# A gated delta-rule decoder layer on one core: the level-64 products of the triangular inverse issued in pairs, gate projections between the groups

## The chip, the cores and the metric

The kernel runs on one core of a Trainium2 chip, in fp32 throughout. The metric is the device time of one execution in microseconds; lower is better.

## The reference

A decoder layer on x of 4 sequences of 256 tokens, width 256: x plus an attention part, plus a cross-attention mix, plus a mixture of experts. The change lies in the attention part, a recurrence over 8 heads of width 128 with two key and value pairs for each token:

```python
def step(state, inp):
    q_t, k_t, v_t, b_t, g_t = inp
    state = state * jnp.exp(g_t)[..., None, None]
    for j in range(nh):                      # nh = 2
        kj = k_t[:, j]
        corr = jnp.einsum('bhk,bhkv->bhv', kj, state)
        u = (v_t[:, j] - corr) * b_t[:, j][..., None]
        state = state + jnp.einsum('bhk,bhv->bhkv', kj, u)
    o_t = jnp.einsum('bhk,bhkv->bhv', q_t, state)
    return (state, o_t)
...
gate = (x @ Wg).reshape(B, L, H, Dh)
o = o * jax.lax.rsqrt(jnp.mean(o * o, axis=-1, keepdims=True) + EPS)
o = o * norm_w * jax.nn.silu(gate)
out = o.reshape(B, L, H * Dh) @ Wo
```

q, k and v are projections of x, each with a causal convolution of 4 taps and a silu.

## The kernel before, in words

The recurrence is worked in chunks of 64 tokens (128 key rows, since each token has two), 16 chunks for each head. In a chunk the dependence of the 128 corrections on each other is a unit triangular 128x128 matrix, and its inverse is needed. The inverse is built by levels. Blocks of 32x32 on the diagonal are inverted on GpSimd. From them TensorE builds blocks of 64 (items p32 and t32: two products), and from those the full 128 (items x32, p64, t64). In the last three, for every chunk, x32 is a turn (transpose) of a 64x64 block, p64 a 64x64 product with that turned block, and t64 a second 64x64 product with the result. Each item comes as n = 0 and n = 1, of eight chunks each; all eight write one PSUM bank, and ScalarE copies the bank out (to XP for x32 and p64, to TT for t64). p64 n waits for the copy of x32 n, and t64 n for the copy of p64 n.

Five engines each run a program of their own, written out by hand and tied by semaphores. `run_heads` walks through steps; in step s, stage A works on head s (projections, convolutions, norms), stage B on head s − 1 (Gram matrices, decays, inverse), stage C on head s − 2 (the scan over the chunks), stage E on head s − 3 (output projection). Steps 3 to 7 hold all four; step 8 has no stage A. A step has 12 slots. In each slot TensorE does one phase of the scan (slots 0, 3, 6, 9: keys times state, L686; then TT products, L700; then outputs, L714 and L715, with the state update, L719), then the fill items of that slot, then a norm (L610) where there is one, then one projection (L581, slots 0 to 9). After slot 11 comes the place `LAST`, and the next step begins with `FIRST`: the Gram matrices (L637) and q times k (L640).

The table `FILL` sets which items stand where, and every engine walks through the same table. Among the items are gate (one half of the gate's projection of the head, L589: two matmuls of 512 columns, then silu on ScalarE, L860), kend (four turns, L642, evacuated by VectorE, L1131), and out (output projection, L749). Fill items take three PSUM banks in turn: an item waits until the item three before it in the order has been evacuated (`bank_free`).

On VectorE a slot is: first tap of the convolution of the projection before (L1053; it waits for ScalarE's copy L836), the scan's part (R, L1153; U, L1161; S, L1170), the two other taps, the fill items. At the end of slot 9 it turns the 32x32 blocks into X1 (L1143), which p32 (L666) reads in slot 10. In step 8, without projections, the threshold search for the cross attention (L1068, L1070) stands ahead of those turns.

An fp32 matmul appears in the trace as two matmul instructions, each with a weight load of its own; a turn appears as one.

Of the kernel before, what the change touches and what calls it, by code (L numbers as in the profile page):

```python
# [17 lines left out]
STEPS = 64  # L18
CH = SEQ // STEPS
# [79 lines left out]
def four(kind):  # L99
# [15 lines left out]
        9: {"B": [("gate", 0)]},  # L115
        10: {"B": [("p32", 0), ("p32", 1)], "E": [("out", 3)]},
        11: {"B": [("t32", 0), ("t32", 1), ("kend", 2)]},
        LAST: {"B": [("x32", 0), ("x32", 1), ("gate", 1), ("p64", 0), ("p64", 1), ("t64", 0), ("t64", 1)]}}
# [43 lines left out]
def attention(nc, ctx, t, dram):  # L162
# [370 lines left out]
    def tensor_program(pe):  # L533
# [80 lines left out]
        def item(kind, n, X):  # L614
# [12 lines left out]
            if kind in ("gram", "qk", "vtok", "kend"):  # L627
# [19 lines left out]
                return  # L647
            if kind == "p32":
# [4 lines left out]
            elif kind == "x32":  # L653
                pe.wait_ge(t32_done, 2 * h + n + 1)
            elif kind == "p64":
                pe.wait_ge(x32_done, 2 * h + n + 1)
            else:
                pe.wait_ge(p64_done, 2 * h + n + 1)
            for k in range(BC // 2):
                m = n * (BC // 2) + k  # L660
                a_m, t_m = aT[:, m // CH, m % CH, :], TT[par][:, m // CH, m % CH, :]
                cols = slice(k * STEPS, (k + 1) * STEPS)
                if kind == "p32":
                    for g in range(2):
                        src, out = slice(2 * g * NB, (2 * g + 1) * NB), slice((2 * g + 1) * NB, (2 * g + 2) * NB)
                        last = mm(bank[out, k * NB:(k + 1) * NB], a_m[src, out], X1[src, m, :], start=True, stop=True)  # L666
                elif kind == "t32":
                    for g in range(2):
                        src, out = slice((2 * g + 1) * NB, (2 * g + 2) * NB), slice(2 * g * NB, (2 * g + 1) * NB)
                        last = mm(bank[out, k * NB:(k + 1) * NB], P32[src, m, :], t_m[src, src], start=True, stop=True)  # L670
                elif kind == "x32":
                    last = nc.tensor.transpose(bank[0:64, cols], t_m[0:64, 0:64], ident[0:64, 0:64])
                elif kind == "p64":
                    last = mm(bank[64:128, cols], a_m[0:64, 64:128], XP[0:64, m, :], start=True, stop=True)  # L674
                else:
                    last = mm(bank[0:64, cols], XP[64:128, m, :], t_m[64:128, 64:128], start=True, stop=True)
            last.then_inc(b_mm, 1)
# [1339 lines left out]
```

## Time and profile before

| | |
|---|---|
| median of 3 runs | 946.26 us (945.72 to 947.09) |
| profiled execution | 951.51 us, span 949.5 us |
| TensorE matmul busy | 849.2 us, 89% of the span |
| TensorE weight load busy | 597.6 us, 63% |
| VectorE busy | 527.4 us, 56% |
| ScalarE busy | 391.3 us, 41% |
| GpSimd busy | 348.5 us, 37% |
| mean granted clock of TensorE | 0.946 |

Times in the trace count from the start of the span. The head loop fills the first two thirds of it; the mixture of experts, the rest. A steady step of the head loop is about 67 us long. Weight loads run beside matmuls, so their busy time does not add to that of the matmuls. In the rows, an idle time in square brackets is what the engine waited directly before the instruction, and the name behind it is what ended the wait; a row without brackets began with no idle time to speak of. The granted clock is 1.00 at 2.4 GHz and 0.50 at 1.2 GHz.

### The profile page before, as it was taken

How to read it: one execution, taken by the hardware profiler on the slowest of the kernel's cores; microseconds unless marked ns; L12 is line 12 of the kernel's file. 1: busy time of each engine (PE TensorE's matmuls, PEld its weight loads, DVE VectorE, ACT ScalarE, POOL GpSimd, SP SyncE). 2: the span in 40 equal slices, each digit the busy share in tenths (PEclk: the TensorE clock that was granted, in tenths of full speed). 3: DMA queues.
4: the chain of work that ended last, by engine and by line, in shares of the span. 5: the costliest groups of instructions: out<-in, count | busy, mean ns of one | idle time of the engine just before them, and what ended most of it. 6: DMA issues, size and time to landing. Idle time of an engine off the chain costs nothing.

```text
span 949.5 us, 16704 instructions
## 1 busy us (share of the span) xinstructions
PE 849.2 (89%) x5816; PEld 597.6 (63%) x5817; DVE 527.4 (56%) x1221; ACT 391.3 (41%) x839; POOL 348.5 (37%) x654
## 2 busy tenths in 40 slices
PE   4869999999999999999999876874999999999992
PEld 3344566766766856866667765763666677667762
DVE  3664747878868868878778764465511111111113
ACT  2736746655654654565565323102222222222220
POOL 0158268357555564573682570003330000000005
PEclk9987999999999999999999995797999999999997
DMA  8221230131031021021201301009563001100104
GB/s 206 73 41 27 72 81 8 17 78 17 9 79 23 11 70 23 13 67 24 51 2 23 90 1 28 1 1 374 213 223 134 28 28 33 33 29 26 33 23 127
DMA packets 102595, 57.91 MB, mean 61 GB/s; under 512 B 64192, under 2 KB 98048, under 8 KB 102528
## 3 DMA queue, kind: packets, MB, share of 16 engines
q1 hardware_dynamic: 99488, 51.62, 19.8%
q0 software_dynamic: 1536, 4.20, 1.4%
q10 hardware_dynamic: 1504, 1.20, 0.4%
q8 instruction: 41, 0.67, 0.3%
q14 instruction: 26, 0.21, 0.1%
HBM read 42.45 MB, written 14.55 MB: 60 GB/s over the span
## 4 chain that ended last, share of the span: by engine, by line
PE 76%; DVE 10%; ACT 6%; issue 4%; POOL 2%; DMA 1%; SPq 0%; POOLq 0%; ACTq 0%; DVEq 0%
PE bank L1598 16%; PE bank L581 13%; PE bank L1643 9%; PE bank L715 3%; PE bank L589 3%; DVE y L1053 3%; PE bank L749 3%; PE bank L640 3%; PE bank L700 3%; PE bank L719 2%; PE bank L714 2%; PE bank L595 2%; PE bank L1630 2%; PE bank L674 2%; PE bank L686 2%
## 5 line engine op out<-in xcount | busy, mean ns | idle before, releaser
L1053 DVE SCALAR_TENSOR_TENSOR y<-bank,cwh,y 128x510 f32<-128x510 f32 (+2 forms) x240 | 177.6, 744 | 78.9 <-ACT y L836 75.2
L581 PE MATMUL bank<-xnT,wbuf 128*128 128x512 f32 x320 | 165.2, 642 | 5.3 <-DVE y L1053 4.7
L1598 PE MATMUL bank<-f_wgu,f_xgT 128*128 x368 | 118.8, 466 | 0.0
L1857 DVE TENSOR_TENSOR f_act<-f_sg,bank 128x352 f32<-128x352 f32 x62 | 32.2, 521 | 143.8 <-PE bank L1598 141.4
L1369 POOL TENSOR_TENSOR term<-inv,blk 128x126 f32<-128x126 f32 (+22 forms) x248 | 87.8, 354 | 43.9 <-DMA blk<-a_blocks 25.1
L1932 POOL DMA_INDIRECT f_back<-slots_y,f_slot x16 | 15.4, 963 | 231.4 <-DMA slots_y<-f_yb 224.8
L581 PEld LDWEIGHTS bank<-xnT,wbuf 128*128 128x128 f32 x320 | 57.4, 199 | 66.8 <-issue 53.7
L1372 POOL TENSOR_TENSOR inv<-inv,term 128x126 f32<-128x126 f32 (+22 forms) x248 | 91.6, 369 | 19.4
L1705 ACT ACTIVATE f_sg<-bank 128x352 f32<-128x352 f32 x62 | 28.7, 464 | 161.0 <-PE bank L1598 152.7
L1643 PE MATMUL bank<-f_wdn,f_actT 128*128 (+1 forms) x372 | 91.5, 388 | 0.9 <-ACT f_actT L1718 0.8
L1598 PEld LDWEIGHTS bank<-f_wgu,f_xgT 128*128 128x128 f32 x368 | 66.2, 190 | 36.8 <-issue 7.6
L836 ACT ACTIVATE y<-bank,cwh 128x512 f32<-128x512 f32 x80 | 54.9, 686 | 74.8 <-PE bank L581 73.3
L1643 PEld LDWEIGHTS bank<-f_wdn,f_actT 128*128 128x128 f32 x372 | 67.9, 189 | 24.5 <-issue 12.0
L1314 POOL TENSOR_TENSOR dx<-dx,minus_beta 128x1024 f32<-128x1024 f32 x8 | 15.2, 1903 | 131.9 <-DVE beta_n L1103 131.9
L930 ACT ACTIVATE vtok<-bank,kn 128x128 f32<-128x128 f32 x128 | 36.5, 369 | 32.6 <-PE bank L645 32.5
L715 PE MATMUL bank<-mq,R 128*128 128x64 f32 x256 | 46.4, 279 | 2.8 <-DVE R L1161 2.8
L1299 POOL TENSOR_TENSOR factor<-factor,masks 128x8 f32<-128x8 f32 x8 | 13.3, 1664 | 96.3 <-DVE factor L1205 96.3
L1598 PE MATMUL bank<-f_wgu,f_x2T 128*128 128x352 f32 x128 | 44.6, 495 | 0.4 <-DVE f_act L1857 0.4
L715 PEld LDWEIGHTS bank<-mq,R 128*128 128x128 f32 x256 | 38.6, 197 | 6.0 <-DVE R L1161 3.0
L1869 DVE COPY f_yb<-bank 128x256 f32<-128x256 f32 x23 | 9.8, 425 | 53.0 <-PE bank L1643 53.0
L700 PEld LDWEIGHTS bank<-R,TT 128*128 128x128 f32 x192 | 25.0, 193 | 22.1 <-issue 19.3
L595 PE MATMUL bank<-gm,masks 64*128 64x512 f32 x64 | 27.5, 687 | 12.1 <-ACT dx L870 8.0
(208 smaller groups left out, 1585.2 us busy)
## 6 DMA issues: line engine op xcount, KB each, us to landing
f_wgu<-in_exp_gu SPq DMA_DIRECT2D x8, 1408.0 KB, 8.6
f_wdn<-in_exp_dn SPq DMA_DIRECT2D x8, 640.0 KB, 9.7
blk<-a_blocks SPq DMA_DIRECT2D x16, 256.0 KB, 3.9
slots_x<-oT SPq DMA_DIRECT2D x24, 128.0 KB, 1.8
f_xg<-slots_x SPq DMA_DIRECT2D x24, 128.0 KB, 2.0
slots_y<-f_yb SPq DMA_DIRECT2D x23, 128.0 KB, 1.7
a_blocks<-aT SPq DMA_DIRECT2D x64, 32.0 KB, 1.6
inverses<-inv SPq DMA_DIRECT2D x16, 128.0 KB, 3.0
```

The costliest lines, as they stand in the source:

```text
L581: last = mm(bankA[p % 2][:, :], wbuf[A.par][:, kt, wblk, :], xnT[:, kt, (p % 2) * 512:(p % 2 + 1) * 512], start=kt == 0, stop=kt == 1)
L595: return mm(bank[:, :], mask("rest" if kind == "dx" else "ones", i * STEPS, STEPS), gm[half_, :, :].rearrange("p n t -> p (n t)"), start=T ...
L700: last = mm(bankC[1][:, b * P:(b + 1) * P], TT[par][:, b, c, :], R[:, b, :] if c else vtok[par][:, b, c, :], start=True, stop=True)
L715: last = mm(out, U[:, b, :], mq[par][:, b, c, :], start=c == 0, stop=True)
L836: a(y[p % 2][:, :, :].rearrange("p b t -> p (b t)"), bankA[p % 2][:, :], ACT.Copy, scale=cwh[A.par][:, cb, 3:4]).then_inc(evac_done, 1)
L930: last = a(vtok[B.par][:, b, c, :], bank[:, c * P:(c + 1) * P], ACT.Copy, scale=kn[:, b * CH + c:b * CH + c + 1])
L1053: v.scalar_tensor_tensor(out=y[p % 2][:, :, k:], in0=src[:, :, 0:SEQ - k], scalar=cwh[A.par][:, cb, 3 - k:4 - k], in1=y[p % 2][:, :, k:], ...
L1369: g.tensor_tensor(step_term, inv[:, 0:r, j:j + 1].to_broadcast([P, r, k]), blk[:, j:j + 1, j + 1:].to_broadcast([P, r, k]), ALU.mult).then ...
L1372: g.tensor_tensor(inv[:, 0:r, j + 1:], inv[:, 0:r, j + 1:], step_term, ALU.add).then_inc(inv_done if j == NB - 2 else inv_step, 1)
L1598: last = mm(gu[c][:, 0:FFH], xt[:, k, :], wgu[:, e, k, at:at + FFH], start=k == 0, stop=k == 1)
L1643: last = mm(dn[par][:, 0:HID], aT[0:rows, par, k, :], wdn[0:rows, e, k, :], start=k == 0, stop=k == FT - 1)
L1857: v.tensor_tensor(av[:, par, half * FFH:(half + 1) * FFH], sg[:, half, :], gu[2 * half + 1][:, 0:FFH], ALU.mult).then_inc(f_act, 1)
```

## The change

The three items of level 64 keep their work, but not their order. x32 1 and p64 0 are issued together, chunk by chunk in turn, and so are p64 1 and t64 0 (`joined`); each pair first makes all the waits of both items, and raises both semaphores at its end. Between the groups stand other items: gate 0 comes from slot 9 to between x32 0 and the first pair, gate 1 stands between the pairs, kend 2 comes from slot 11 to between the second pair and t64 1. The other engines follow the same table: ScalarE copies the gate's half 0 in `LAST`, and VectorE evacuates kend 2 in `LAST`.

```diff
-        9: {"B": [("gate", 0)]},
+        9: {},
         10: {"B": [("p32", 0), ("p32", 1)], "E": [("out", 3)]},
-        11: {"B": [("t32", 0), ("t32", 1), ("kend", 2)]},
-        LAST: {"B": [("x32", 0), ("x32", 1), ("gate", 1), ("p64", 0), ("p64", 1), ("t64", 0), ("t64", 1)]}}
+        11: {"B": [("t32", 0), ("t32", 1)]},
+        LAST: {"B": [("x32", 0), ("gate", 0), ("x32", 1), ("p64", 0), ("gate", 1), ("p64", 1), ("t64", 0), ("kend", 2), ("t64", 1)]}}
+JOIN = {("x32", 1): ("p64", 0), ("p64", 1): ("t64", 0)}
...
+        def joined(first, second, X):
+
+            banks = [bankB[bank_of(kind, X.h, n)] for kind, n in (first, second)]
+            for kind, n in (first, second):
+                bank_free(pe, kind, X.h, n)
+                level_ready(kind, n, X.h)
             for k in range(BC // 2):
...
+                one_, two_ = level(*first, X, k, banks[0]), level(*second, X, k, banks[1])
+            one_.then_inc(b_mm, 1)
+            two_.then_inc(b_mm, 1)
...
                         for kind, n in items:
-                            item(kind, n, stages[stage])
+                            if (kind, n) in JOIN:
+                                joined((kind, n), JOIN[kind, n], stages[stage])
+                            elif (kind, n) not in JOIN.values():
+                                item(kind, n, stages[stage])
```

`level` and `level_ready` hold the products and the waits that stood in `item` before:

```python
if kind == "x32":
    last = nc.tensor.transpose(bank[0:64, cols], t_m[0:64, 0:64], ident[0:64, 0:64])
elif kind == "p64":
    last = mm(bank[64:128, cols], a_m[0:64, 64:128], XP[0:64, m, :], start=True, stop=True)
else:
    last = mm(bank[0:64, cols], XP[64:128, m, :], t_m[64:128, 64:128], start=True, stop=True)
```

The order on TensorE in slots 9 and 10 of step 6, before (L686 is the scan's product of slot 9, L589 gate 0, L666 level 32's first products):

```order
L686 MATMUL bank<-S,kT 128x128 x4
L589 MATMUL bank<-xnT,wg 128x512 x2
L610 MATMUL bank<-osq,masks 32x128 x4
L581 MATMUL bank<-xnT,wbuf 128x512 x2
L700 MATMUL bank<-R,TT 128x128 x4
L666 MATMUL bank<-X,aT 32x32 x32
```

And in the changed kernel, whose line numbers are other ones (L707 is L686 of before, L676 is L666):

```order
L707 MATMUL bank<-S,kT 128x128 x4
L611 MATMUL bank<-osq,masks 32x128 x4
L582 MATMUL bank<-xnT,wbuf 128x512 x2
L721 MATMUL bank<-R,TT 128x128 x4
L676 MATMUL bank<-X,aT 32x32 x32
```

The gate's two matmuls have gone from between the scan's product and the products of level 32.

The order on TensorE at the end of the same step, before (from t32, L670, to the next head's Gram matrices, L637):

```order
L670 MATMUL bank<-TT,P 32x32 x32
L642 MATMUL bank<-masks,kT 128x128 x4
L610 MATMUL bank<-osq,masks 32x128 x8
L672 MATMUL bank<-masks,TT 64x64 x16
L589 MATMUL bank<-xnT,wg 128x512 x2
L674 MATMUL bank<-XP,aT 64x64 x16
L676 MATMUL bank<-TT,XP 64x64 x16
L637 MATMUL bank<-kraw 128x128 x16
```

And in the changed kernel (L680 is t32, L682 the turns, L684 p64, L686 t64, L643 kend, L590 gate); each pair of alternating rows stands eight times, and only its first and last are shown:

```order
L680 MATMUL bank<-TT,P 32x32 x32
L611 MATMUL bank<-osq,masks 32x128 x8
L682 MATMUL bank<-masks,TT 64x64 x8
L590 MATMUL bank<-xnT,wg 128x512 x2
L682 MATMUL bank<-masks,TT 64x64
L684 MATMUL bank<-XP,aT 64x64
...
L590 MATMUL bank<-xnT,wg 128x512 x2
L684 MATMUL bank<-XP,aT 64x64
L686 MATMUL bank<-TT,XP 64x64
...
L643 MATMUL bank<-masks,kT 128x128 x4
L686 MATMUL bank<-TT,XP 64x64 x8
L638 MATMUL bank<-kraw 128x128 x16
```

A second gate projection and the turns of kend now stand among the level's items, and four of its six items are issued in turns instead of in blocks.

## Rows read from the trace of the kernel before

**Rows 1.** Timeline of TensorE, slots 9 and 10 of a steady step: start, duration, instruction.

```profile
441.18 1.05 PE L686 MATMUL bank<-S,kT 128*128 128x128 f32 x8
442.07 1.88 PE L589 MATMUL bank<-xnT,wg 128*128 128x512 f32 x4
443.88 0.43 PE L610 MATMUL bank<-osq,masks 128*32 128x128 f32 x8
444.24 1.98 PE L581 MATMUL bank<-xnT,wbuf 128*128 128x512 f32 x4
...
447.04 1.20 PE L666 MATMUL bank<-X,aT 32*32 32x32 f32 x64
```

**Rows 2.** Timeline of VectorE at the same place.

```profile
442.10 0.75 DVE L1053 SCALAR_TENSOR_TENSOR y<-bank,cwh,y 128x510 f32<-128x510 f32 x1 [0.27 <-ACT y L836]
...
445.24 1.42 DVE L1143 STREAM_TRANSPOSE X<-TT 32x512 f32<-32x512 f32 x2
446.98 0.75 DVE L1053 SCALAR_TENSOR_TENSOR y<-bank,cwh,y 128x510 f32<-128x510 f32 x1 [0.32 <-ACT y L836]
```

**Rows 3.** Timeline of TensorE, end of the same step.

```profile
450.96 1.20 PE L670 MATMUL bank<-TT,P 32*32 32x32 f32 x64
452.10 0.66 PE L642 MATMUL bank<-masks,kT 128*128 128x128 f32 x4
452.68 0.65 PE L610 MATMUL bank<-osq,masks 128*32 128x128 f32 x16
453.26 1.08 PE L672 MATMUL bank<-masks,TT 64*64 64x64 f32 x16
454.27 1.98 PE L589 MATMUL bank<-xnT,wg 128*128 128x512 f32 x4
456.18 2.08 PE L674 MATMUL bank<-XP,aT 64*64 64x64 f32 x32
458.10 2.05 PE L676 MATMUL bank<-TT,XP 64*64 64x64 f32 x32
460.07 2.94 PE L637 MATMUL bank<-kraw 128*128 128x128 f32 x24
```

**Rows 4.** Timeline of ScalarE at the same end: copies of t32 0 and p64 1.

```profile
452.09 0.38 ACT L942 ACTIVATE TT<-bank 32x256 f32<-32x256 f32 x1
...
458.29 0.59 ACT L946 ACTIVATE XP<-bank 64x512 f32<-64x512 f32 x1 [0.34 <-PE bank L674]
```

**Rows 5.** The instructions of line 551: duration min/median/max, first and last start.

```profile
L551 PE MATMUL bank<-wab,xnT x64: 270/281/303, 16.1 to 19.5; 128*64 128x24 f32 x64
```

**Rows 6.** Timeline of TensorE in step 8.

```profile
579.88 1.92 PE L666 MATMUL bank<-X,aT 32*32 32x32 f32 x64 [7.37 <-DVE X L1143]
...
588.89 1.11 PE L642 MATMUL bank<-masks,kT 128*128 128x128 f32 x4
589.93 1.91 PE L672 MATMUL bank<-masks,TT 64*64 64x64 f32 x16
591.77 3.78 PE L589 MATMUL bank<-xnT,wg 128*128 128x512 f32 x4
595.49 3.35 PE L674 MATMUL bank<-XP,aT 64*64 64x64 f32 x29
598.53 0.36 PE L676 MATMUL bank<-TT,XP 64*64 64x64 f32 x1
598.63 0.31 PE L674 MATMUL bank<-XP,aT 64*64 64x64 f32 x1
...
603.83 0.66 PE L728 MATMUL bank<-osq,masks 128*32 128x256 f32 x4 [1.63 <-ACT osq L887]
```

**Rows 7.** TensorE by stretches: from:to and length, busy (instructions), clock, DMA share, GB/s.

```profile
54.00:55.00 1.00, 0.00 (x0) 1.00 0.00 0
...
590.00:603.00 13.00, 12.21 (x85) 0.50 0.00 0
606.00:610.00 4.00, 4.00 (x27) 0.84 0.03 6
```

More of the change, by code:

```diff
@@ L647, in item, with level_ready @@
                 return
+            level_ready(kind, n, h)
+            for k in range(BC // 2):
+                last = level(kind, n, X, k, bank)
+            last.then_inc(b_mm, 1)
+        def level_ready(kind, n, h):
             if kind == "p32":
@@ L658, in item @@
                 pe.wait_ge(p64_done, 2 * h + n + 1)
-            for k in range(BC // 2):
[L660 to L676, printed above, removed]
@@ L677, in item, with level @@
-            last.then_inc(b_mm, 1)
+        def level(kind, n, X, k, bank):
+            par, m = X.par, n * (BC // 2) + k
+            a_m, t_m = aT[:, m // CH, m % CH, :], TT[par][:, m // CH, m % CH, :]
+            cols = slice(k * STEPS, (k + 1) * STEPS)
+            if kind == "p32":
+                for g in range(2):
+                    src, out = slice(2 * g * NB, (2 * g + 1) * NB), slice((2 * g + 1) * NB, (2 * g + 2) * NB)
+                    last = mm(bank[out, k * NB:(k + 1) * NB], a_m[src, out], X1[src, m, :], start=True, stop=True)
+            elif kind == "t32":
+                for g in range(2):
+                    src, out = slice((2 * g + 1) * NB, (2 * g + 2) * NB), slice(2 * g * NB, (2 * g + 1) * NB)
+                    last = mm(bank[out, k * NB:(k + 1) * NB], P32[src, m, :], t_m[src, src], start=True, stop=True)
+            elif kind == "x32":
+                last = nc.tensor.transpose(bank[0:64, cols], t_m[0:64, 0:64], ident[0:64, 0:64])
+            elif kind == "p64":
+                last = mm(bank[64:128, cols], a_m[0:64, 64:128], XP[0:64, m, :], start=True, stop=True)
+            else:
+                last = mm(bank[0:64, cols], XP[64:128, m, :], t_m[64:128, 64:128], start=True, stop=True)
+            return last
```

## The prediction, made before the changed kernel ran

> **What bounds the kernel now.** I read the waits of TensorE first, then its timeline in one step of the head loop, then VectorE's and ScalarE's timelines at the same places. The reader should see in the steady step (step 6 here, where head 5 is in stage B) that TensorE runs from instruction to instruction with almost no idle mark: neither the rows of slots 9 and 10 [rows 1] nor those of the step's end [rows 3] carry one. So a microsecond added to TensorE's queue there is a microsecond of the kernel, unless another engine is about to stop TensorE anyway. The second thing to see is where that is nearly so: VectorE in slot 9 waits 0.27 us for the copy of projection 8 and 0.32 us for that of projection 9, and has no idle mark between, before the two turns L1143 that give X1 [rows 2]. They end at about 446.66 (the next VectorE row starts at 446.98 after 0.32 us of idle), and L666, the first product of level 32, which reads X1, starts at 447.04 [rows 1]. TensorE reaches L666 only 0.38 us after VectorE has finished X1. That margin decides what slot 9 can give back.
>
> **The change part by part.** Steady step first (steps 1 to 7; step 8 has no projections and is costed apart).
>
> *Slot 9 loses gate 0.* It takes 443.88 − 442.07 = 1.81 us of TensorE [rows 1]. Without it, TensorE would stand at L666 at 447.04 − 1.81 = 445.23. But X1 does not come earlier: VectorE's row at 442.10 waits for ScalarE's copy of projection 8, which lies before the gate in TensorE's order, and from there VectorE works without a gap to 446.66 [rows 2]. Allowing 0.05 us for the release (an estimate, a third of the 0.19 that a copy needs to start behind its product), L666 starts at about 446.70: I book −0.35 us instead of −1.81, and expect a new wait of about 1.45 us in front of L666 on X1. Queued behind it are out 3, the o products and level 32's second half, all needed for the step's end. VectorE itself gains its 0.32 us of idle (projection 9 is ready early), so U, and what follows it, moves forward with TensorE by the same 0.35.
>
> *Slot 11 loses kend 2:* 452.68 − 452.10 = −0.58 us [rows 3]. What is late next is the t32 copy that the first turn (x32) needs: its second half starts at 452.09 and takes 0.38 [rows 4], so it ends at 452.47, now 0.35 earlier, 452.12. TensorE arrives at 453.26 − 0.35 − 0.58 = 452.33. Covered, by 0.1 to 0.2 us; no wait booked.
>
> *Gate 0 enters the last place:* gate 1 there takes 456.18 − 454.27 = 1.91 us, against the 1.81 of slot 9 [rows 1, 3]; I read the 0.1 as the change of the array's tile shape from and to 64x64. +1.91.
>
> *Pair one, turns x32 1 with products p64 0.* Both take their rows from partitions 0 to 63, and write columns 0 to 63 and 64 to 127. Now: 16 turns take 454.27 − 453.26 = 1.01 us, 63 ns each; the 32 instructions of p64 (two per fp32 matmul) take 1.92 us, 60 ns each [rows 3]. So eight turns and sixteen of p64 cost 0.50 + 0.96 = 1.46. The nearest row for two tiles that share rows and differ in columns is L551: 64 instructions, alternately to columns 0 to 63 and 64 to 127, started between 16.1 and 19.5, so 54 ns from start to start, although each streams only 24 columns [rows 5]. That is what loading 64 columns of weights costs; loads of such tiles followed one another. With 24 loads at about 56 ns the pair takes 1.35 us: −0.1. The bounds: no overlap at all 1.46, full overlap 16 x 60 ns = 0.96. I take 1.35, because L551 is the same geometry.
>
> The Trainium skill (TensorE: Matmul & The Clock Gate, Part 3, The mechanism) says that a weight load overlaps running matmuls only where the row group differs. By that rule pair one gains next to nothing, and pair two gains.
>
> *Pair two, p64 1 with t64 0.* Rows 0 to 63 to columns 64 to 127, and rows 64 to 127 to columns 0 to 63: nothing shared, and different banks. Now it costs half of 460.07 − 456.18, 1.95 us [rows 3]. Two rows say that it overlaps. The 32x32 products alternate between tiles with no common row or column, and 64 of them take 452.10 − 450.96 = 1.14 us, 18 ns each [rows 3], less than a third of the 60 ns of the 64-column ones. And in step 8, where p64 ends and t64 begins, their records alternate 50 to 100 ns apart at half clock [rows 6]. If both tiles run at their own 60 ns, 32 instructions take 16 x 60 = 0.96; I take 1.0. −0.95. Bounds: 0.96 and 1.95.
>
> *kend 2 and t64 1.* kend 2 costs 0.58 to 0.6 again. t64 1 needs the copy of p64 1, whose group now ends together with its partner's. The copy starts 0.19 us after its product (458.29 against 458.10) and takes 0.59 [rows 3, 4]; with the release, 0.87 from the end of the pair. kend 2 covers 0.60 of it; I book 0.87 for both. Gate 1 waits for gate 0's bank to be copied, which a copy of some 0.6 us manages behind pair one; kend 2's evacuation on VectorE is needed by the second gram only.
>
> Sum of a steady step: −0.35 − 0.58 + 1.91 − 0.1 − 0.95 + 0.87 = **+0.80 us**; what follows (gram and the gate of the output behind ScalarE's last copies) moves along with the end of t64. Step 1 has its X1 wait and its end built the same way; seven steps give +5.6.
>
> *Step 8.* L666 already waits 7.37 us for X1 there [rows 6], since VectorE does the threshold search first. Gate 0 ahead of it was free and now is not. The clock stands at 0.50 throughout the end of the step [rows 7], so 1.2 GHz: kend 1.04, 16 turns 1.84, gate 3.72, and p64 with t64 about 6.6 (595.49 to about 602.1, where the wait of 1.63 us before L728 at 603.83 begins) [rows 6]. At that clock throughout: −1.04 for kend, +0.1 wait, +3.72 gate, −0.1 for pair one, −1.6 for pair two (half of 6.6 to 1.7), +1.04 kend again, and some 0.5 for copies not covered: +2.6. But the clock came back after 606, once large matmuls ran close together [rows 7], and now two gates stand near each other where one did. If full clock returns with the end of gate 0, gate 1 takes 1.91 instead of 3.72 and the rest halves: the group ends near 600.4 instead of 602.1, and the 3.2 us from 603.83 to about 607 save another 1.5: −3.2. I cannot tell where it returns; I book −1.4, between the middle and the good end, because a run of two gates is far denser than what stood there.
>
> Total +5.6 − 1.4 = +4.2 us. The terms come from the profiled execution (951.51 us, span 949.5); I add them to the median of the runs, 946.26: **950.5 us**.
>
> **The rivals.**
> - *Both pairs overlap fully.* For it: nothing but the weight loads stands against pair one, and their price may be lower when a partner streams 64 columns. Then pair one takes 0.96 and pair two 0.96, 0.43 less: 0.37 per step, 7 x 0.37 = +2.6; with step 8 from −3.2 to +2.6 that is 945.7 to 951.5, with my −1.4 it is 947.5. The Trainium skill (TensorEngine Tiling, Key Properties) states that different tiles execute weight loads and matmuls in parallel, which is this rival. Chance 0.14.
> - *Neither pair overlaps,* because each change of tile costs what the overlap gives. 0.1 + 0.95 more per step: 7 x 1.85 = +13; step 8 keeps its 1.6 too and comes to about 0: 959. Against it: the alternating rows at half clock. Chance 0.07.
> - *Clock falls in the new wait.* 1.45 us of idle before small products might lower the granted clock. One fall over a gate's length costs 3.72 − 1.91 = 1.8 us [rows 3, 6]; three of them give 956. Against it: between 54 and 55 TensorE stood idle inside a much longer wait and kept 1.00 [rows 7]. Chance 0.05.
> - *Faster: X1 doesn't hold L666.* If VectorE gets through slot 9 by 1.46 us earlier, the whole 1.81 comes back and a step is +0.80 − 1.46 = −0.66: −4.6 − 1.4, 940.2. It decides in one place: the change gains as soon as slot 9 gives back more than 1.15 us per step. For it: the trace shows no wait at L666 now. Against it: VectorE's unbroken rows to 446.66 [rows 2]. Chance 0.08.
> - The forecast itself: 0.66, own range 948.7 to 954.5.
>
> **How the numbers follow.** About 0.2% (1.9 us) is what a measurement of this kernel can tell from no change. Slower takes the forecast but for 0.05 (clock back early and a little more overlap), half of the first rival, the second and the third: 0.77. Same takes 0.05 and half of the rest of the first rival: 0.12. Faster: the fourth rival and the low end of the first: 0.11. The range 946.6 to 958.0 leaves out the fourth rival and the upper part of the second.
>
> **What would show it.** In the profile after: idle of 1.2 to 1.6 us before the 32x32 products L676, on X1, in steps 1 to 7, and their start only 0.3 to 0.4 us earlier in the step; the stretch of x32 1 with p64 0 at 1.3 to 1.4 us and that of p64 1 with t64 0 at 1.0 to 1.1; about 0.3 us before t64 1 on the copy of p64 1; steps longer by 0.8 us; in step 8 the granted clock back before 606. The forecast is wrong if L676 shows no wait, if pair one takes under 1.1 us, or if pair two takes over 1.5.

## The result, and the profile after

The changed kernel takes **989.14 us** (median of 4 runs, 987.04 to 991.97), the kernel before in the same comparison 945.99 us (943.99 to 947.09, 4 runs). The ratio is **1.0448, 95% interval [1.0402, 1.0494]**: 43 us slower, where 4.2 were forecast. The direction was as forecast, the size was not, and the time lies far outside the range.

The profiled execution after (987.04 us, span 984.9) is the fastest of its four; that of before (951.51, span 949.5) lies above all four of the comparison. So these two traces show only 35.4 of the 43 us. In the changed file the lines have moved: L707 was L686, L590 was L589 (gate), L582 was L581 (projection), L611 was L610, L721 was L700, L676 and L680 are the products of level 32 (L666, L670), L682 the turns (L672), L684 p64 (L674), L686 t64 (L676), L643 kend (L642), L638 the gram (L637), L1167 the turns that give X1 (L1143), L749 the norm that ends step 8's last place (L728), L596 the products behind ScalarE's dx (L595).

TensorE's timeline in step 6, against [rows 1] and [rows 3]: start, duration, instruction, idle before it.

```profile
464.32 1.05 PE L707 MATMUL bank<-S,kT 128*128 128x128 f32 x8
...
...
469.94 1.20 PE L676 MATMUL bank<-X,aT 32*32 32x32 f32 x64 [1.41 <-DVE X L1167]
...
476.13 1.98 PE L590 MATMUL bank<-xnT,wg 128*128 128x512 f32 x4
478.05 0.24 PE L682 MATMUL bank<-masks,TT 64*64 64x64 f32 x1
478.22 0.32 PE L684 MATMUL bank<-XP,aT 64*64 64x64 f32 x2
478.47 0.24 PE L682 MATMUL bank<-masks,TT 64*64 64x64 f32 x1
...
481.48 1.98 PE L590 MATMUL bank<-xnT,wg 128*128 128x512 f32 x4
483.39 0.27 PE L684 MATMUL bank<-XP,aT 64*64 64x64 f32 x1
483.40 0.27 PE L686 MATMUL bank<-TT,XP 64*64 64x64 f32 x1
...
484.47 0.66 PE L643 MATMUL bank<-masks,kT 128*128 128x128 f32 x4
485.30 1.11 PE L686 MATMUL bank<-TT,XP 64*64 64x64 f32 x16 [0.18 <-ACT XP L970]
```

Three things are to be seen. The gate is gone from slot 9, and the forecast wait of 1.41 us stands before L676. **Pair one takes 481.48 − 478.05 = 3.43 us**: in each of its eight rounds the turn starts 0.43 us after the one before. Pair two takes 484.47 − 483.39 = 1.08 us, with its two tiles 6 to 10 ns apart.

From L707 to the gram L638 (464.32 to 486.35) the step takes 22.03 us, where before it took 18.89 (441.18 to 460.07): +3.14 at full clock.

TensorE by stretches, against [rows 7]: from:to and length, busy (instructions), granted clock, DMA share, GB/s. First what recurs in every steady step, then the fall in step 2, then step 8. A fall is a stretch in which the granted clock is down.

```profile
357.00:360.00 3.00, 3.00 (x9) 0.50 1.20 252
500.00:504.00 4.00, 4.00 (x13) 0.57 0.16 50
...
179.00:190.00 11.00, 11.00 (x110) 0.53 0.01 1
...
603.00:627.00 24.00, 16.68 (x174) 0.51 0.09 17
627.00:630.00 3.00, 3.00 (x21) 0.96 0.00 0
```

All but the last of these stretches run at 1.2 GHz and not at 2.4. The step from one L596 row to the next (behind dx) takes 71.68 us (283.20 to 354.88). In before it takes 66.87 where no such fall lies in it and 68.57 where one does, so a fall costs 1.7 us; 66.87 + 3.14 + 1.7 = 71.7, and every one of these steps (3 to 6) has one. Before has such a fall at the same place in three of its steps only (1, 3 and 4).

Step 8, against [rows 6]:

```profile
612.30 1.92 PE L676 MATMUL bank<-X,aT 32*32 32x32 f32 x64 [6.45 <-DVE X L1167]
...
622.43 3.78 PE L590 MATMUL bank<-xnT,wg 128*128 128x512 f32 x4
...
629.64 3.68 PE L590 MATMUL bank<-xnT,wg 128*128 128x512 f32 x4
...
637.91 0.64 PE L749 MATMUL bank<-osq,masks 128*32 128x256 f32 x8 [1.63 <-ACT osq L911]
```

From L676 to L749 step 8 takes 637.91 − 612.30 = 25.61 us, before 603.83 − 579.88 = 23.95: +1.66, not −1.4. Gate 0 ran at half clock; the clock rose behind it at 626.3 and was full for nearly all of pair one (626.15 to 629.64, 0.43 us a round as in the steady steps), fell again for gate 1, which took 3.61 us, and was back for pair two.

By these rows the work adds 7 x 3.14 + 1.66 = 23.6 us. The rest of the 43 is not work of TensorE.

### The profile page after: what moved, and what is told of

Its sections match the earlier page's. It is cut to its first block, busy times and chain, and to the rows that moved or that the text cites. A ratio compares the mean times of both kernels' runs of the same rounds, so it can differ in the third digit from the quotient of the medians.

```text
span 984.9 us, 16704 instructions
## 1 busy us (share of the span) xinstructions
PE 875.1 (89%) x5816; PEld 606.7 (62%) x5817; DVE 520.6 (53%) x1221; ACT 391.7 (40%) x839; POOL 341.2 (35%) x654
## 4 chain that ended last, share of the span: by engine, by line
PE 74%; DVE 12%; ACT 6%; issue 4%; POOL 2%; DMA 2%; SPq 0%; POOLq 0%; ACTq 0%; DVEq 0%
PE bank L1622 16%; PE bank L582 11%; PE bank L1667 8%; PE bank L590 4%; DVE y L1077 4%; PE bank L736 3%; PE bank L770 3%; PE bank L641 3%; PE bank L684 2%; PE bank L740 2%; PE bank L735 2%; PE bank L1654 2%; PE bank L721 2%; PE bank L596 2%; PE bank L682 2%
## 5 line engine op out<-in xcount | busy, mean ns | idle before, releaser
L582 PE MATMUL bank<-xnT,wbuf 128*128 128x512 f32 x320 | 162.2, 632 | 7.4 <-DVE y L1077 6.8
L582 PEld LDWEIGHTS bank<-xnT,wbuf 128*128 128x128 f32 x320 | 55.7, 193 | 66.5 <-issue 51.3
L736 PE MATMUL bank<-mq,R 128*128 128x64 f32 x256 | 48.5, 289 | 3.1 <-DVE R L1185 3.1
L1155 DVE TENSOR_TENSOR kend<-bank,sh 128x512 f32<-128x512 f32 x24 | 16.4, 685 | 57.8 <-PE bank L643 57.8
L590 PE MATMUL bank<-xnT,wg 128*128 128x512 f32 x64 | 41.5, 784 | 0.0
L721 PEld LDWEIGHTS bank<-R,TT 128*128 128x128 f32 x192 | 25.6, 196 | 23.2 <-issue 19.3
```

Source lines behind the costliest of these rows:

```text
L582: last = mm(bankA[p % 2][:, :], wbuf[A.par][:, kt, wblk, :], xnT[:, kt, (p % 2) * 512:(p % 2 + 1) * 512], start=kt == 0, stop=kt == 1)
L590: last = mm(bank[:, :], wg[B.par][:, kt, :], xnT[:, kt, i * 512:(i + 1) * 512], start=kt == 0, stop=kt == 1)
L721: last = mm(bankC[1][:, b * P:(b + 1) * P], TT[par][:, b, c, :], R[:, b, :] if c else vtok[par][:, b, c, :], start=True, stop=True)
L736: last = mm(out, U[:, b, :], mq[par][:, b, c, :], start=c == 0, stop=True)
```

## The experiments

Times are medians; each ratio is to runs of the kernel before on the same chip. A run marked "extra work" issues instructions whose results nobody reads.

| run | us | ratio [95%] |
|---|---|---|
| e1, pair two only | 971.07 | 1.0230 [1.0189, 1.0272] |
| e2, moves only | 987.97 | 1.0446 [1.0375, 1.0518] |
| e3, pair one's turns as matmuls | 969.22 | 1.0216 [1.0160, 1.0272] |
| e4, four turns, four products | 982.27 | 1.0332 [1.0276, 1.0388] |
| e5, gate 0 back, both pairs | 995.83 | 1.0508 [1.0477, 1.0540] |
| e6, before with gate 0 moved | 969.65 | 1.0235 [1.0182, 1.0288] |
| e7, e1 with out 3 ahead of p32 | 961.69 | 1.0142 [1.0102, 1.0182] |
| e8, gate 0 back, pair two only | 959.37 | 1.0131 [1.0100, 1.0162] |
| e9, e10, turns against other tiles | 1017.70, 1008.32 | one run each |
| e11, work between the pairs | 964.17 | 1.0193 [1.0152, 1.0234] |
| e12, pair one as matmuls alone | 948.76 | 1.0008 [0.9985, 1.0032] |
| e13, e1 with the wait filled | 960.86 | 1.0123 [1.0081, 1.0166] |
| e14, before with a late X1 | 975.97 | 1.0246 [1.0190, 1.0301] |
| e15, before, step 8's wait filled | 945.86 | 0.9962 [0.9934, 0.9989] |
| e16, and the expert part's | 938.76 | 0.9880 [0.9839, 0.9921] |
| e17, changed, wait filled | 981.71 | 1.0359 [1.0292, 1.0427] |
| e18, e3 with the wait filled | 955.74 | 1.0074 [1.0039, 1.0109] |

### What pair one costs

**e1** joins pair two alone, **e2** neither:

```
-JOIN = {("x32", 1): ("p64", 0), ("p64", 1): ("t64", 0)}
+JOIN = {("p64", 1): ("t64", 0)}        # e1
+JOIN = {}                              # e2
```

> The changed kernel with pair one split again: x32 1 and then p64 0, each as a block of eight; the order of the items and pair two stay. Theory A (alternating a turn with a product stops the array at each of the switches): the stretch of x32 1 and p64 0 falls from 3.43 us to 1.46, a step of 71.68 us to about 69.7 or less, and the kernel from 989 us to 953 to 965. Rival (the loss lies in the moved items and in what they do to the granted clock): the stretch shortens too, but the kernel stays above 975 us.

> The changed kernel with both pairs split, so that only the places of gate 0, kend 2 and the level's items differ from the kernel before. Theory A: +1.6 us per step over before (slot 9 gives 0.35 back, slot 11 0.58, the last place takes 1.91 and 0.6), 957 to 963 us. Rival (the moved items carry the loss): 975 us and more.

Neither came out as theory A had it. e1's 971 us lies between A's range and the rival's; splitting the pair took 2.2% off, more than the 14 us that eight stretches shorter by 1.80 us make. And e2, which has no pair at all, is as slow as the changed kernel (988 us): there the rival's forecast was met. So the alternating pair can't be the whole loss; the moved items cost by themselves, and most of that must be something other than work.

**e4** keeps both pairs, but pair one changes from turns to products and back only every fourth:

```
-            for k in range(BC // 2):
-                one_, two_ = level(*first, X, k, banks[0]), level(*second, X, k, banks[1])
+            grain = 4 if first[0] == "x32" else 1
+            for k0 in range(0, BC // 2, grain):
+                for k in range(k0, k0 + grain):
+                    one_ = level(*first, X, k, banks[0])
+                for k in range(k0, k0 + grain):
+                    two_ = level(*second, X, k, banks[1])
```

> The changed kernel with pair one in groups of four: four turns, four products, four turns, four products. If a switch costs (theories A and B), 3 switches instead of 15 leave the stretch at 1.46 us plus 0.4 to 0.5, about 1.9 us, and the kernel at 962 to 977 us. If turns or products are slow for another reason as long as the two items share the stretch (rival C, for instance the two banks), it stays near 3.4 us and 987 us.

The stretch came out as expected; the kernel is 5 us above its range.

TensorE's timeline, e1:

```profile
465.33 0.63 PE L682 MATMUL bank<-masks,TT 64*64 64x64 f32 x8
465.89 1.14 PE L684 MATMUL bank<-XP,aT 64*64 64x64 f32 x16
466.96 1.98 PE L590 MATMUL bank<-xnT,wg 128*128 128x512 f32 x4
```

And e4:

```profile
403.38 0.41 PE L682 MATMUL bank<-masks,TT 64*64 64x64 f32 x4
403.72 0.68 PE L684 MATMUL bank<-XP,aT 64*64 64x64 f32 x8
404.32 0.41 PE L682 MATMUL bank<-masks,TT 64*64 64x64 f32 x4
404.66 0.67 PE L684 MATMUL bank<-XP,aT 64*64 64x64 f32 x8
405.27 1.12 PE L590 MATMUL bank<-xnT,wg 128*128 128x512 f32 x2
```

The same 24 instructions take 1.63 us with one switch from turn to product or back, 1.89 with three and 3.43 with fifteen: 0.13 us a switch by either difference ((1.89 − 1.63)/2, (3.43 − 1.63)/14). None of the three is shorter than the 1.46 us of turns and products one behind the other: turns and products did not overlap.

**e3** writes the eight turns of x32 1 as fp32 matmuls of the same 64x64 block with the identity, same tiles, same alternation:

```
+                if n == 1:
+                    last = mm(bank[0:64, cols], t_m[0:64, 0:64], ident[0:64, 0:64], start=True, stop=True)
```

> The changed kernel with the eight turns of x32 1 issued as fp32 matmuls by the identity (two instructions each) instead of as transposes; pair one alternates as in the changed kernel, tiles and banks are the same. Theory A (the switch between transpose and matmul stops the array): 32 instructions at 54 to 60 ns, 1.7 to 1.9 us instead of 3.43, kernel 962 to 977 us. Rival B (alternating two tiles that share the rows 0 to 63 stops the array, whatever the kind of instruction): the stretch stays at 3.4 us or grows, the kernel stays at 987 us or more.

TensorE's timeline, e3 (L683 the former turns, L687 p64):

```profile
462.34 0.27 PE L683 MATMUL bank<-masks,TT 64*64 64x64 f32 x1
462.35 0.27 PE L687 MATMUL bank<-XP,aT 64*64 64x64 f32 x1
462.45 0.22 PE L683 MATMUL bank<-masks,TT 64*64 64x64 f32 x1
```

The next gate starts at 463.42, so the pair takes 1.08 us though it now has 32 instructions instead of 24, less than the 1.7 to 1.9 expected. Both tiles take rows 0 to 63, and yet start 6 to 10 ns apart every 58 ns, as those of pair two do, which share nothing. Shared rows are no hindrance; the switch between transpose and product is. Why it is isn't shown.

**e9** and **e10** put unused products (extra work, L701) between the turns, of the turns' own tile in e9 (`q = slice(0, 64)`), in e10 of rows 64 to 127 to columns 0 to 63 (`q = slice(64, 128)`); p64 0 follows in a block:

```
+                    one_ = level(*first, X, k, banks[0])
+                    mm(banks[1][0:64, cols], a_m[q, q], t_m[q, q], start=True, stop=True)
```

> The changed kernel, but the turns of x32 1 alternate with eight added products of the same tile (rows and columns 0 to 63; their results are not used), and p64 0 follows as a block. If every switch between a turn and a product in 64x64 tiles stops the array, whichever the tile (theory A), the alternating stretch takes 3.4 us again, and 1.07 us of p64 0 come behind it. If the stop comes from a transpose and a product sharing rows but not columns (theory F), the stretch takes 8 x 63 + 16 x 60 ns = 1.5 us.

> As the run with the same tile, but the added products read rows 64 to 127 and write columns 0 to 63. Theory A: 3.4 us for the alternating stretch. Theory F (a transpose and a product sharing rows): 1.5 us or less, down to 1.1.

TensorE's timeline, e9:

```profile
422.04 0.24 PE L682 MATMUL bank<-masks,TT 64*64 64x64 f32 x1
...
422.47 0.24 PE L682 MATMUL bank<-masks,TT 64*64 64x64 f32 x1
```

And e10:

```profile
413.91 0.24 PE L682 MATMUL bank<-masks,TT 64*64 64x64 f32 x1
414.08 0.33 PE L701 MATMUL bank<-TT,aT 64*64 64x64 f32 x2
414.33 0.24 PE L682 MATMUL bank<-masks,TT 64*64 64x64 f32 x1
```

A round takes 0.42 to 0.43 us in the same tile, in one with other rows and in one with other columns (the changed kernel). So the stop comes in each of these three arrangements; a product with both other rows and other columns was not tried.

### What the wait for X1 does to the clock

By its rows e1 has 3.14 − 1.80 (pair one) = 1.34 us more work a step than before, 9.4 in seven, and 1.8 less than before in step 8 (22.12 us against 23.95 from the 32x32 products to the norm); it cost 2.3%, 22 us. **e6** is the kernel before with gate 0 moved behind x32 1, next to gate 1, and nothing paired:

```
-        9: {"B": [("gate", 0)]},
+        9: {},
-        LAST: {"B": [("x32", 0), ("x32", 1), ("gate", 1), ("p64", 0), ...
+        LAST: {"B": [("x32", 0), ("x32", 1), ("gate", 0), ("gate", 1), ("p64", 0), ...
```

> The kernel before with one edit: gate 0 goes from slot 9 to directly before gate 1 in the last place. No pairs, kend 2 stays in slot 11. By the work alone: 1.46 us more in each of steps 1 to 7 and 3.7 in step 8, 960 to 964 us. Theory D adds falls of the clock after the new idle, 970 to 990 us, with at least two stretches of 7 us or more at half clock that begin within 5 us of the 32x32 products of steps 1 to 7. Rival (sparse work of the reordered last place lets it fall): no such stretches, 960 to 964 us.

Its wait for X1 is 1.41 us and its work 1.46 a step, 10 in seven, with 0.3 less than before in step 8 (23.61 us against 23.95); it is 22 slower. TensorE's timeline, then its stretches, e6:

```profile
239.79 1.20 PE L666 MATMUL bank<-X,aT 32*32 32x32 f32 x64 [1.41 <-DVE X L1143]
```

```profile
235.00:240.00 5.00, 3.59 (x35) 1.00 0.14 21
242.00:255.00 13.00, 13.00 (x122) 0.50 0.01 1
```

Full clock up to the wait and for 1.5 us behind it, then half for 13 us, although TensorE works without a gap there. That happened in three of the seven steps (again at 317 to 330 and 528 to 542), about 6 us each. Work and these falls make more than 22, because steps 1 to 6 lack the three short falls that before has.

**e14** leaves TensorE's order alone and makes X1 late, by a memset of 1700 columns on VectorE (extra work) ahead of its two turns:

```
+            if B.h < HEADS - 1:
+                v.memset(junk[:, :], 0.0)
```

> The kernel before, with a VectorE memset of 1700 columns ahead of the turns that give X1, in steps 1 to 7; nothing on TensorE is moved. TensorE gets an idle of 1.1 to 1.5 us before the 32x32 products, 8 to 10 us in all: 954 to 957 us by that alone. Theory D: long stretches at half clock begin behind it in some of the steps, 960 to 975 us. Rival (missing gate in slot 9, or gates together in the last place, make them): none, 954 to 957 us.

TensorE's timeline and stretches, e14:

```profile
173.90 1.20 PE L667 MATMUL bank<-X,aT 32*32 32x32 f32 x64 [1.42 <-DVE X L1147]
```

```profile
176.00:189.00 13.00, 13.00 (x126) 0.50 0.01 2
...
459.00:473.00 14.00, 14.00 (x124) 0.52 0.01 2
```

Six waits of 1.42 us and one of 1.24 are 10 us; the kernel lost 2.46%, 23 us. The rest is the clock: in three of the steps (534 to 548 as well) it stays at half for 13 to 14 us, which cost 6 to 7 each in the profiled execution, whose span is 29 us above that of before. **The wait itself makes the clock fall**, with no instruction of TensorE moved. The memset was not run without the wait; e13 and e7 below, which have no memset, say the same from the other side.

**e13** is e1 with the first matmul of projection 9 issued twice (extra work of 0.86 us in the wait, in steps 1 to 7), so that 0.55 us of idle is left:

```
+            if p == 9 and A.h:
+                mm(bankA[p % 2][:, :], wbuf[A.par][:, 0, wblk, :], xnT[:, 0, 512:1024], start=True, stop=True)
```

> The kernel of the first experiment (pair two only, 971 us) with the first matmul of projection 9 issued twice, in steps 1 to 7: 0.86 us more work of TensorE per step, in a bank that is overwritten, standing in the 1.41 us of idle. If idle lets the clock fall (theory D): long stretches at half clock after the 32x32 products become fewer (three of them, 34 us, in that kernel's profile), 958 to 966 us, faster with more work. If the order of the items does (rival): 970 to 973 us.

Stretches of e1, then of e13:

```profile
241.00:255.00 14.00, 14.00 (x125) 0.51 0.01 1
```

```profile
241.00:255.00 14.00, 13.82 (x203) 1.00 0.01 2
```

With more to do it is 10 us faster than e1 (1.0123 against 1.0230). **e7** reaches the same without extra work: out 3 (0.97 us) ahead of p32 instead of behind it.

```
-        10: {"B": [("p32", 0), ("p32", 1)], "E": [("out", 3)]},
+        10: {"E": [("out", 3)], "B": [("p32", 0), ("p32", 1)]},
```

> The kernel of the first experiment (pair two only) with out 3 ahead of p32 in slot 10, so that in steps 3 to 7 about 0.97 us of output projection fills the idle in front of the 32x32 products, which starts no earlier. By the work alone nothing more than 0.5 to 1.0 us per step is won, 963 to 968 us. Theory D: the long falls in steps 3 to 7 go (idle 0.45 instead of 1.41), 950 to 960 us. Rival: they stay, 964 to 971 us.

The idle is 0.54 us from step 3 on. Steps 1 and 2, where 1.23 and 1.41 us are left, have a fall each, of 7 and 10 us, step 3 one of 7, steps 4 to 7 none. 9 us faster than e1, 2 above its range.

**e5** puts gate 0 back into slot 9 and keeps both pairs, in the order x32 0, pair one, gate 1, pair two, kend 2, t64 1:

```
-        9: {},
+        9: {"B": [("gate", 0)]},
```

> The changed kernel with gate 0 in slot 9 again; both pairs as in the change, so pair one (3.43 us) now stands directly behind x32 0 and waits for its copy. Theory D (the idle of 1.41 us before the 32x32 products, followed by small work, is what lets the granted clock fall for 7 to 17 us at a time): no idle before the 32x32 products in steps 1 to 7, no fall of the clock between slot 10 and the end of a step, and 962 to 970 us: about 2.3 us of extra TensorE time in each of 8 steps over before (3.43 for 1.46, 0.75 for the wait, less 0.9 in pair two). Rival E (the turns alternating with products are what lets the clock fall): falls remain in or behind the last place, 975 us or more.

TensorE's timeline, e5:

```profile
262.34 0.21 PE L682 MATMUL bank<-masks,TT 64*64 64x64 f32 x1 [1.39 <-ACT XP L968]
```

The wait at p32 is gone, but gate 0 was also the cover for ScalarE's copy of x32 0, which p64 0 reads: 1.39 us of idle stand before pair one, in small work, and in each of the seven steps the clock falls there, for 7 to 10 us. The time is rival E's and not theory D's, but D's condition, no idle, wasn't met: wait and stops stand at one place here, and the run doesn't separate them. It is the slowest of those in which only order and pairing changed. Gate 0 ahead of pair one, as the cover of that copy, was a good part of the change.

### Versions in between

**e8** (as e5, pair two only), **e12** (gate 0 in slot 9; x32 0, gate 1, pair one as matmuls, kend 2, p64 1, t64 0, t64 1) and **e11** (kend 1, kend 2 and out 3 moved between the groups, both pairs, pair one as matmuls) look for an order without any of the waits:

```
+        LAST: x32 0, x32 1, p64 0, gate 1, [p64 1 + t64 0], kend 2, t64 1                      (e8)
+        LAST: x32 0, gate 1, [x32 1 + p64 0], kend 2, p64 1, t64 0, t64 1                      (e12)
+        LAST: x32 0, gate 1, [x32 1 + p64 0], kend 1, kend 2, [p64 1 + t64 0], out 3, t64 1    (e11)
```

> Gate 0 in slot 9, no pair one, pair two, kend 2 between pair two and t64 1; last place x32 0, x32 1, p64 0, gate 1, p64 1 with t64 0, kend 2, t64 1. Theory A with D: no fall of the clock behind slot 10, step 0.2 us shorter than before (pair two saves 0.9; 0.3 wait for x32 0's copy and 0.3 for p64 1's are new, and two changes of tile shape), 943 to 948 us. Rival (kend 2 or pair two in the last place costs): 955 us or more.

> A version made to keep what works: gate 0 in slot 9, the turns of x32 1 as matmuls paired with p64 0, pair two, and kend 1, kend 2 and out 3 moved between the groups to cover the copies (last place: x32 0, gate 1, pair one, kend 1, kend 2, pair two, out 3, t64 1). Work: about 0.6 us less than before in each step with an output projection (steps 3 to 8), 0.2 more in steps 1 and 2, where out 3 is missing and t64 1 waits 0.8 us. If no idle of over 0.4 us stands beside small work in steps 3 to 7, the clock keeps there, and the kernel takes 939 to 945 us; if idle in steps 1 and 2 lets it fall there, up to 7 us more.

> Pair one alone, with its turns as matmuls, gate 0 in slot 9: last place x32 0, gate 1, pair one, kend 2, p64 1, t64 0, t64 1 in blocks. Work: within 0.1 us of before per step; 944 to 949 us if theory D holds and the idle of some 0.25 us before p64 1 is too short to matter; 955 us or more if even that lets the clock fall.

TensorE's timeline, e8 (its gate behind p64 0 took 3.78 us), then e11:

```profile
250.80 1.74 PE L684 MATMUL bank<-XP,aT 64*64 64x64 f32 x16 [0.72 <-ACT XP L968]
```

```profile
324.03 0.24 PE L687 MATMUL bank<-XP,aT 64*64 64x64 f32 x1 [1.87 <-DVE kend L1158]
```

e8 and e11 missed their ranges, e12 came out as expected, which is no gain; each lost at a hand-over. In e8 p64 0 waits 0.72 us for a copy, and the clock falls there in each of the seven steps, for 3 to 7 us. In e11 kend 1 and kend 2 hold their banks while VectorE is in its threshold search, and pair two's bank comes 1.87 us late in steps 2 to 7. e12 equals the kernel before: waits of 0.18 us (ScalarE's copy) and 0.50 (kend's bank) took what pair one gave.

### What the 43 us are made of

**e17** is the changed kernel, **e18** is e3, each with e13's extra matmul in the wait for X1.

> The changed kernel in full, with the first matmul of projection 9 issued twice in steps 1 to 7, so that TensorE works 0.86 us of the 1.4 it waited for X1. It is the same unused matmul as in the run with one pair. Theory A (work adds 23 to 24 us by the rows, and the rest of the 43 is clock that falls because of the wait for X1): the clock's part goes, and the time comes to 967 to 973. Theory B (the 15 stops in pair one lower the clock as well, seen as short falls of some 4 us at the start of the next step at 285, 357, 429 and 500): those falls stay, about 2 us each, and the time is 975 to 982. If the work by the rows were wrong and the clock a follower, the time would stay at 985 to 990.

> The changed kernel with the turns of x32 1 written as matmuls with the identity (pair one then has no stop and took 1.08 us) and the same filled wait. This is the change with nothing in it but the work that my sum counted: +0.80 per step, less 0.27 for pair one, about +0.5, so +4 in seven steps and step 8 between -3 and +3. If stop and clock are the whole of what the prediction missed: 947 to 956. If something else in the moved pieces costs as well (the gates next to each other, the uncovered copies): over 960.

By the ratios, with 946 us for the kernel before:

- e18, the change with neither stop nor long wait: 0.74%, **7 us** [4, 10]. This is what my sum was about (4.2). Its steps took 1.58 us more than before and its step 8 2.6 less.
- e17 less e18, the stops in pair one: 2.85%, **27 us**. Of that the rows give 7 x (3.43 − 1.08) = 16.5, and 2.5 more in step 8, where pair one takes 3.6 us in the one and 1.1 in the other. The rest is clock: gate 1 of step 8 took 3.4 us against 1.9, and e17 has seven short falls at 1.7 us each in steps 1 to 7 where e18 has two.
- The changed kernel less e17, what filling 0.86 us of the wait saves without removing any work: 0.89%, **8 us**. The intervals of the two ratios overlap, so its size is rough; the two profiles differ by 3.2 us, and their steady steps not at all (71.63 against 71.68), only step 2, whose long fall e17 has not (69.34 against 73.80).

This is one way to take the change apart, and the shares hold for it alone. From e2 the way is another: the moves cost 42 us with no stop in them, pair two takes about 20 off (e1), pair one adds about 20 again. The profile of e2, the slowest of its four (1001 us, the others 987 to 989), has five falls of 10 to 21 us behind waits for X1; that of the changed kernel two, of 7 and 10. So stops and long falls replace each other in part, and the 43 us are not a sum of fixed costs.

The stretches of e17, in which pair one and the gate behind it lie, and of e18, 290 us over four steps:

```profile
408.00:411.00 3.00, 3.00 (x25) 0.54 0.03 8
479.00:483.00 4.00, 4.00 (x36) 0.57 0.00 0
```

```profile
264.00:554.00 290.00, 271.21 (x2396) 1.00 0.18 38
```

So e17's theory B held in the time and in the falls' length, not in their place: each step still has a short fall, which with matmul turns is gone (what e18 has are two at the wait for dx, in steps 1 and 2; before has three there). The fall at 408 begins right behind pair one (its last turn in that step starts at 406.35, gate 1 at 406.78), in the changed kernel only 18.5 us behind pair one, at the wait for dx. That the stops bring the falls behind pair one is shown by e18, and that they make those at dx more frequent by the counts (four in steps 3 to 6 of the changed kernel, two before, none in e18); why they come at one place or the other isn't.

e18's steps are 68.45 us (276.05 to 344.50), 1.58 more than 66.87, where +0.5 follows from my terms. From the scan's product to the gram its rows give +0.79 (449.03 to 468.71, 19.68 us against 18.89). The other 0.8 stands behind, where the gram waits for VectorE's aT. GpSimd, VectorE and TensorE of e18, then TensorE of before:

```profile
470.34 1.04 POOL L1315 TENSOR_TENSOR gm<-g_sb,masks 128x512 f32<-128x512 f32 x1
470.38 2.08 DVE L1225 SCALAR_TENSOR_TENSOR og<-oT,normw,gate 128x1024 f32<-128x1024 f32 x1 [2.17 <-ACT osq L916]
473.12 1.16 PE L640 MATMUL bank<-kraw 128*128 128x128 f32 x8 [1.47 <-DVE aT L1146]
```

```profile
463.69 1.16 PE L637 MATMUL bank<-kraw 128*128 128x128 f32 x8 [0.67 <-DVE aT L1117]
```

og takes 2.08 us instead of before's 1.28, with GpSimd's product gm beside it. The other traces follow the overlap: 1.28 us with no gm beside it (before, the changed kernel), 1.39 with 0.31 us of gm (e6), 1.50 with 0.42 (e1), 1.94 with 0.85 (e7), 2.07 with 0.98 (e3). No run moved gm alone. The step's end, when it comes earlier, runs into gm, and so e1, e13 and e18 take 68.45 us and e3 68.47, though pair one takes 1.63 us in the first two and 1.08 in the others: what pairing saved there, VectorE took back.

### The clock where the change is not

**e15** and **e16** take the kernel before and give TensorE unused 512-column matmuls while it waits: eight in step 8 ahead of p32, and in e16 eleven more ahead of the expert part's first turns.

```
+                if s == HEADS and slot == 10:
+                    pe.wait_ge(conv_step, 30 * HEADS)
+                    for _ in range(8):
+                        mm(bankA[0][:, :], wbuf[1][:, 0, 0, :], xnT[:, 0, 0:512], start=True, stop=True)
...
+        for _ in range(11):
+            mm(gu[0][:, :], ident, masks[:, 0:512], start=True, stop=True)
```

> The kernel before, with eight unused matmuls of 512 columns (6.9 us at full clock) in step 8 while TensorE waits 7.4 us for X1. Theory D: the 34 us at half clock from there on shrink to under 10, and the kernel takes 934 to 940 us. Rival (the sparse items themselves bring the clock down): 944 to 948 us.

> As the run with step 8 kept busy, with eleven more unused matmuls of 512 columns in the idle of 10.4 us before the expert part's first turns. If the same holds there: another 3 to 7 us less, 928 to 936 us. Rival: the same as the run with step 8 alone.

TensorE's timeline, e15, against [rows 6], and its stretches:

```profile
577.15 1.20 PE L666 MATMUL bank<-X,aT 32*32 32x32 f32 x64
...
584.04 1.98 PE L589 MATMUL bank<-xnT,wg 128*128 128x512 f32 x4
```

```profile
573.00:593.00 20.00, 18.30 (x260) 0.99 0.03 8
...
634.00:648.00 14.00, 6.88 (x20) 0.53 1.05 409
```

And the stretches of e16:

```profile
573.00:592.00 19.00, 17.13 (x247) 1.00 0.03 8
...
630.00:654.00 24.00, 19.40 (x84) 0.99 0.93 355
```

L666 to the gate takes 6.9 us instead of 11.9, and 34 us at half clock are gone. e15 gains 0.4%, less than its expectation. In its profile the clock is low elsewhere: 14 us between 540 and 572, where before has 7, and 27 us in the expert part, where before has 20. e16 keeps the expert part's clock, and gains **1.2%: it beats both kernels**, with 19 matmuls nobody needs, though 3 us short of its expectation too.

## Why the prediction was wrong, step by step

- *Slot 9, −0.35, and a wait of 1.45 us on X1.* Right: −0.24 (5.62 against 5.86 from L707 to L676) and 1.41.
- *Slots 10 and 11, −0.58.* Right: 5.63 against 6.22 from p32 to x32.
- *Gate 0, +1.91.* Right: 1.92.
- *Pair one, 1.35 us, bounds 0.96 to 1.46.* **This step failed.** It took 3.43, outside both bounds, +2.08 a step against the term, where I expected overlap and the rows show a stop of 0.13 us at each of fifteen switches. I bounded it from below by full overlap and from above by none, and took for granted that alternating costs nothing. Its nearest row, L551, alternated products with products. No row of before alternates 64x64 turns with products, so the upper bound had no basis, and among my signs of being wrong only a pair that was too fast stood. The argument on shared rows fell as well: e3 shows two such tiles overlapping fully. The rule of the Trainium skill (TensorE: Matmul & The Clock Gate, Part 3, The mechanism), that a weight load overlaps running matmuls only where the row group differs, does not describe e3, where the row group is the same; the measurement decides. The first rival's rule (the Trainium skill, TensorEngine Tiling (Array Packing), Key Properties), that different tiles can load weights and multiply in parallel, agrees with e3 (1.08 us). The first rival as priced, 0.96 for pair one with turns, did not come about.
- *Pair two, 1.0.* Right: 1.08.
- *kend 2 and the wait for p64 1, 0.87.* Right: 0.83, with 0.18 of wait.
- *Step 8, −1.4.* Wrong in sign but within its −3.2 to +2.6: +1.66. The clock did come back with the end of gate 0, as I had hoped, but fell again behind the stops of pair one, for gate 1. Without stops it stayed: e18 takes 21.36 us there (590.07 to 611.43), −2.6, and e1 22.12, −1.8. So this term failed by pair one too.
- *What follows moves along with the end of t64.* It did in the changed kernel (+3.14 us to the gram, +3.1 in the step less its fall). Once the stops are gone it doesn't: in e18 the gram's wait for VectorE grew by 0.8.
- *The clock.* **The second failure.** I gave it 0.05 and priced a fall at one gate's length, 1.8 us. A long fall lasts 10 to 14 us, so it costs 5 to 7; e6 and e14 have three of them each. I argued against it from one stretch inside a longer wait that kept 1.00 [rows 7]. That told nothing of the stretch behind a wait: in e6 as well the clock is 1.00 through the wait and 0.50 from 1.5 us behind it on.
- *Slips.* 0.05 us is a quarter of 0.19, not a third. By the shares named, slower adds to 0.80 and same to 0.09, not 0.77 and 0.12. Nothing rests on either.

Without the stop and most of the wait the total would have stood roughly: e18 ended at 955.7, inside the range, though partly by luck, since its steps cost twice the +0.80 and its step 8 gave more back than I booked. By the mechanism this was the rival "neither overlaps, because each change costs", but what changes is the operation, not the tile: pair two changes tile as often and is fast.

What stays open: why the long fall follows the wait in some steps and not in others (of seven nearly equal waits it came after two in the changed kernel, after three in e1); why e2, which has no stops, is as slow as the changed kernel and e6 isn't (e2 also moves kend 2, and five falls of 10 to 21 us stand in its profile, which is that of its slowest execution); why a switch between transpose and product stops TensorE; and whether og and gm really slow each other.

## What to carry to other kernels

Pack small fp32 work into quadrants only with instructions of one kind: here a transpose among products stopped TensorE each time, and writing it as a matmul with the identity made it free here. When an edit opens a wait on the engine that bounds the kernel, look at the granted clock behind the wait, not in it, and move whole work into it (out 3 did as well as a dummy). Bound an unseen alternation from above by something worse than its two parts in sequence.

## What was not expected of the hardware

- A switch between a 64x64 transpose and a 64x64 fp32 product cost 0.13 us on TensorE, in the same quadrant, with other rows and with other columns alike.
- Products of two 64x64 tiles overlapped fully though they share their rows: 32 instructions in 1.08 us.
- A wait of 1.4 us in otherwise unbroken work was followed, in three of seven steps (e1, e6, e14), by 10 to 14 us at 1.2 GHz, in work that fills TensorE; where 0.37 to 0.55 us of idle were left (e7, e13, e17, e18), a fall of 7 us followed at once in three of twenty-six steps.
- VectorE's og took 1.28 us alone and 2.08 with a GpSimd product of 1.04 us beside it.
- Nineteen matmuls without use made the kernel 1.2% faster.
